# Attention and a mixture of experts on one core: all products of the attention in 64 x 32 tiles of the array

## The chip, the core and the metric

The kernel runs on one core of a Trainium2 chip. The metric is the device time of one execution in microseconds: 1344.58 before, the median of three runs (1342.93 to 1349.27).

## The reference

For 16 batches of 256 rows of 128 features:

```
x = x + tanh(g_xattn) * attn(layernorm(x), ctx)   # 16 heads of 8, softmax over 1601 keys per batch
x = x + tanh(g_ffn)   * ffn(layernorm(x))         # 8 experts 128 -> 512 -> 128, best 2 per token

attn: qh = q Wq[h]; kh = ctx Wk[h]; vh = ctx Wv[h]
      out_h = softmax(0.125 * qh kh^T) vh;  concat(out_h) Wo^T
ffn:  probabilities of the 2 best experts, normalised; sum of cw_e * (gelu(x w1_e^T + b1_e) w2_e^T + b2_e)
```

Everything is float32. The scores are large, so the maximum over the keys of every row and head is subtracted before the exponential.

## The kernel before

**Packing.** Queries and keys are split into three bfloat16 parts each. Six products of parts, of 8 features each, stand under one another on 48 partitions (`MAXROW`), for one head from partition 0 and for another from partition 64 (`RG` = 2 row halves of the array). Three more rows carry the negative maximum, so that a product of 51 rows gives score minus maximum.

**Work of a group.** Four heads are a group (`NG` = 4 groups a batch, 64 in all; `JJ` = 2 heads on each row half). A group needs:
- its maxima first: a *window* (`window`, L782) is a product of 128 queries with 402 keys (`WIN`), written into one bank of PSUM. The two row halves write the two banks of one buffer (`mxp`, `MX_BUFS` = 2), and DVE takes both banks in one reduction (`maximum`, L1540, L1546). `NMX` = 16 such pairs are a group. Then DVE joins them to `nmx` (L1554), POOL splits that in three (`split_maxima`), PE turns it (`turn_maxima`, L827), ACT copies it and two DMAs put it under the queries (`place_half`).
- 13 *units*, one per 128 keys (the last has 65). `scores` (L758) makes four products of 128 keys x 256 queries, two heads a bank, into a ring of three banks `st`, which also serves all smaller products; ACT makes the exponentials into SBUF (L1077); `weighted` (L803) multiplies them, four heads as four strips of 32 columns over all 128 key rows, by the values and a column of ones, and adds up in one bank `pv` over two groups. The values are float32, and each float32 product shows as two passes in the trace.

**Order.** Every engine runs a list written out by hand. PE's goes unit by unit: scores of this unit with the first pair of windows beside them, then further windows, the weighted values of the unit two before (`LAG`), then the chores that the tables at L96 to L106 put at this unit (keys', values' and queries' products of later batches, the attention's projection and the routing of the batch before), and last the windows of the second list. `WINDOWS_AT` (L108; `FIRST_WINDOWS_AT` for batch 0) says how many pairs are made at each unit, before and after the chores; `FIRST` pairs are made before the first unit and `LEAD` is how far the windows are ahead of the units. DVE takes reductions and its small work in the same order, ACT exponentials and copies. PE waits for a free `mxp` buffer (`s_red`), for a free ring bank (`freed`) and for the exponentials (`s_exp`); DVE waits for the windows (`s_mxp`), ACT for the scores (`s_st`) and for the weighted values (`s_pv`) before it writes over old exponentials.

After the last unit comes the expert stage: 43 blocks of rows, two products each with gelu between, and the sum of the results. The change does not touch it, except for the last transpose of the weighted values.

## Time and profile before

| | |
|---|---|
| median of the runs | 1344.58 us |
| span of the profiled execution, which is all that the page gives of its time | 1360.3 us |
| PE busy | 1289.7 us (95%), 14041 matmuls |
| DVE busy | 1157.6 us (85%) |
| ACT busy | 1094.7 us (80%) |
| POOL busy | 546.7 us (40%) |
| mean granted TensorE clock | 0.975 |

PE is TensorE's matmuls and PEld its weight loads, DVE is VectorE, ACT ScalarE, POOL GpSimd. A matmul's end is modelled, and matmuls are pipelined: PE's busy share says that something was in the array, not that it ran at its peak. Distances between starts say more.

### The profile page before, as it was taken

The page shows a single profiled execution, that of the slowest core. Times are in us where ns is not written, and L with a number is a line of the kernel's source. Part 1 is how long each engine was busy: PE and PEld are TensorE (multiplying, and loading weights), DVE is VectorE, ACT ScalarE, POOL GpSimd, SP SyncE. Part 2 cuts the span into 40 slices and gives each one's busy share as a digit, 9 for nine tenths or more (in the row PEclk, how much of TensorE's full clock was granted, in tenths as well). Part 3 has the DMA queues.
Part 4 walks back from the last instruction along what each step waited for, and adds up shares of the span by engine and source line. Part 5 has one row for each costly group of instructions (what it writes and reads, how often), then busy time and mean ns, then how long its engine had stood idle before and what let it go on. Part 6 is the DMA issues. An engine that isn't in the chain of part 4 may idle for free.

```text
span 1360.3 us, 38009 instructions
## 1 busy us (share of the span) xinstructions
PE 1289.7 (95%) x14041; PEld 627.0 (46%) x14041; DVE 1157.6 (85%) x2268; ACT 1094.7 (80%) x2190; POOL 546.7 (40%) x1208
## 2 busy tenths in 40 slices
PE   4899999999999999999999999999999999998992
PEld 2243444444444444444444444444444433497882
DVE  7897999999999999999999999999999999355334
ACT  1487898988889888898989898888989888864561
POOL 3231426262626262535353444444453512145441
PEclk7698999999999999999999999999999999999997
DMA  3232121212121212121222222222211110386886
GB/s 91 76 86 82 45 67 51 70 47 75 46 78 42 83 35 66 52 64 54 64 59 60 63 58 66 58 64 58 67 52 39 49 40 6 98 258 196 252 262 231
DMA packets 61077, 112.67 MB, mean 83 GB/s; under 512 B 13052, under 2 KB 36476, under 8 KB 60748
## 3 DMA queue, kind: packets, MB, share of 16 engines
q1 hardware_dynamic: 54043, 97.67, 24.6%
q0 software_dynamic: 4320, 8.99, 2.0%
q10 hardware_dynamic: 2529, 3.58, 0.8%
q8 instruction: 112, 1.84, 0.6%
q14 instruction: 73, 0.60, 0.2%
HBM read 52.77 MB, written 13.71 MB: 49 GB/s over the span
## 4 chain that ended last, share of the span: by engine, by line
PE 75%; DVE 16%; SPq 3%; issue 3%; DMA 1%; ACT 1%; POOL 0%; POOLq 0%; ACTq 0%; DVEq 0%
PE pv L821 27%; PE st L772 14%; PE mxp L794 13%; DVE mx L1546 13%; PE st L1038 5%; PE mxp L1048 4%; PE st L879 4%; PE st L888 2%; SPq L401 2%; PE st L900 1%; PE st L851 1%; PE st L923 1%; PE st L863 1%; PE st L933 1%; DVE x_sb L1741 1%
## 5 line engine op out<-in xcount | busy, mean ns | idle before, releaser
L1546 DVE TENSOR_REDUCE mx<-mxp 128x2 f32<-128x804 f32 x1024 | 985.2, 987 | 71.1 <-PE mxp L794 60.8
L1077 ACT ACTIVATE arena<-st 128x512 f32<-128x512 f32 (+1 forms) x1664 | 892.2, 595 | 88.8 <-PE st L772 82.2
L821 PE MATMUL pv<-arena 128*32 128x256 f32 x6656 | 535.6, 394 | 0.5 <-ACT pv_sb L1084 0.4
L794 PE MATMUL mxp<-kpack,qpack 48*128 48x402 bf16 x2048 | 457.0, 344 | 16.2 <-DVE mx L1546 14.8
L772 PE MATMUL st<-qpack,kpack 51*128 51x256 bf16 (+1 forms) x3328 | 449.2, 273 | 2.4 <-DMA qpack<-mxT 2.1
L772 PEld LDWEIGHTS st<-qpack,kpack 51*128 51x128 bf16 (+1 forms) x3328 | 199.4, 97 | 202.4 <-ACT arena L1077 108.0
L794 PEld LDWEIGHTS mxp<-kpack,qpack 48*128 48x128 bf16 x2048 | 142.6, 93 | 167.0 <-DVE mx L1546 94.3
L821 PEld LDWEIGHTS pv<-arena 128*32 128x32 f32 x6656 | 131.6, 108 | 177.0 <-issue 89.3
L659 POOL CAST mxs<-nmx 128x8 bf16<-128x8 f32 x64 | 12.4, 193 | 263.3 <-DVE nmx L1554 263.2
L1218 ACT ACTIVATE arena<-st,bias 128x256 f32<-128x256 f32 (+1 forms) x172 | 74.1, 438 | 54.7 <-PE st L1038 38.4
L702 POOL DMA_INDIRECT results<-ysb,idx x71 | 68.9, 971 | 89.2 <-DVE ysb L1683 58.2
L692 POOL DMA_INDIRECT rows<-xrow,pos x64 | 66.2, 1034 | 95.3 <-DVE pos L1403 80.0
L1038 PE MATMUL st<-xT,arena 128*128 128x256 f32 (+1 forms) x344 | 93.0, 353 | 12.1 <-ACT xT L1205 7.9
L1048 PE MATMUL mxp<-arena 128*128 128x128 f32 x568 | 90.8, 275 | 0.0
L1048 PEld LDWEIGHTS mxp<-arena 128*128 128x128 f32 x568 | 85.4, 191 | 5.6
L583 POOL TENSOR_TENSOR tmp<-rstd 128x2 f32<-128x2 f32 x93 | 18.1, 195 | 151.9 <-DVE rstd L1276 147.0
L1675 DVE TENSOR_TENSOR ysb<-mxp,arena 128x256 f32<-128x256 f32 (+1 forms) x43 | 16.3, 378 | 72.5 <-PE mxp L1048 65.8
L879 PE MATMUL st<-arena,wk_sb 128*128 128x400 f32 (+1 forms) x126 | 60.5, 566 | 5.7 <-DMA arena<-in_ctxT 5.7
L888 PE MATMUL st<-wv_sb,arena 128*128 128x128 f32 (+1 forms) x416 | 62.2, 289 | 0.0
L888 PEld LDWEIGHTS st<-wv_sb,arena 128*128 128x128 f32 (+1 forms) x416 | 49.6, 187 | 25.1 <-ACT arena L1119 13.1
L1038 PEld LDWEIGHTS st<-xT,arena 128*128 128x128 f32 x344 | 52.1, 191 | 17.4 <-ACT xT L1205 11.7
L634 POOL TENSOR_TENSOR ksp<-kf,ksp 128x400 bf16<-128x400 f32 (+1 forms) x60 | 56.9, 949 | 4.8
(194 smaller groups left out, 908.7 us busy)
## 6 DMA issues: line engine op xcount, KB each, us to landing
kpack<-ksp SPq DMA_DIRECT2D x750, 50.0 KB
arena<-in_w12T SPq DMA_DIRECT2D x43, 576.0 KB
arena<-in_ctxT SPq DMA_DIRECT2D x15, 800.5 KB, 4.5
qpack<-qsp SPq DMA_DIRECT2D x187, 32.0 KB
xblk<-rows SPq DMA_DIRECT2D x28, 132.0 KB
rows<-in_pads SPq DMA_DIRECT2D x8, 264.0 KB
arena<-results SPq DMA_DIRECT2D x8, 256.0 KB, 6.9
arena<-results ACTq DMA_DIRECT2D x8, 256.0 KB, 7.2
```

What stands on the lines that cost most here:

```text
L692: eng.indirect_dma_start(rows, bass.IndirectOffsetOnAxis(ap=pos[:, k, t:t + 1].bitcast(U32), axis=0), xrow[:, t, k, :], None).then_inc(don ...
L702: eng.indirect_dma_start(results, bass.IndirectOffsetOnAxis(ap=idx[:, i % IDX_BUFS, j:j + 1].bitcast(U32), axis=0), ysb[:, i % YS_BUFS, j, ...
L772: ins = eng.matmul(ring[i][0:n, jj * N:(jj + 1) * N], kpack[rows, b % 2, g * JJ + jj, kt * P:kt * P + n], qpack[rows, b % 2, g * JJ + jj, ...
L794: eng.matmul(mxp[pair % MX_BUFS][:, rg, 0:WIN], qpack[rows, b % 2, g * JJ + jj, t * P:(t + 1) * P], kpack[rows, b % 2, g * JJ + jj, WSTART ...
L821: ins = eng.matmul(pv[32 * j:32 * j + 32, 0:N], vaug[0:n, b % 2, kt, at:at + 32], pt[0:n, (2 * u + rg) % PT_BUFS, jj * N:(jj + 1) * N], st ...
L879: eng.matmul(dst[:, 0:kn], wk_sb[:, :], ctx_sb[:, b % 2, k0:k0 + kn], start=True, stop=True).then_inc(s_kp, 1)
L888: ins = eng.matmul(ring[i][0:n, t * D:(t + 1) * D], ctx_sb[:, b % 2, (t0 + t) * P:(t0 + t) * P + n], wv_sb[:, :], start=True, stop=True)
L1038: eng.matmul(hp[q % HP_BUFS][:, 0:n], w1[:, i % W_BUFS, c * P:(c + 1) * P], xT[:, i % 2, 0:n], start=True, stop=True).then_inc(s_hp, 1)
L1048: ins = eng.matmul(yp[i2 % 2][:, j * D:(j + 1) * D], hf[:, f % RING, j * P:(j + 1) * P], w2[:, i2 % W_BUFS, c2 * D:(c2 + 1) * D], start=(c ...
L1077: eng.activation(pt[0:n, c % PT_BUFS, :], ring[bank_of["S", u, p]][0:n, :], ACT.Exp, scale=SCALE).then_inc(s_exp, 1)
L1218: eng.activation(hf[:, q % RING, 0:n], hp[q % HP_BUFS][:, 0:n], ACT.Gelu_apprx_tanh, bias=bias[:, i % BIAS_BUFS, c:c + 1]).then_inc(s_hg, 1)
L1546: eng.tensor_reduce(mx[:, tj, w, :], mxp[windows_done % MX_BUFS][:, :, 0:WIN], AX.X, ALU.max).then_inc(s_red, 1)
```

## The change

- The tile of the array is named at every product. `strips` cuts a product into pieces of 32 output columns, each with its own load. Scores and windows become products of 64 x 32 tiles, on either row half; the products over 128 rows (keys, values, queries, projection, routing) become strips of 128 x 32.
- The weighted values are cut into the two halves of the 128 keys (`HALVES`), each in 64 x 32 tiles, and each half adds up in its own bank `pv[h]`. ACT copies both banks, and `turn_heads` transposes and adds them by two products with the identity, where it used the transpose mode.
- A window is 512 keys and one bank. Three make 1536 keys; the last 65 keys of all four head-and-half combinations of a row half go into one bank together (`REST`). `mxp` is three single banks, and DVE reduces each bank by itself: 13 pairs a group (`NMX`), 26 reductions.
- `s_mxp`, `s_st` and `s_pv` become two semaphores each, one for a row half. The tables of the order are written anew; `FIRST` goes from 24 to 17 and `LEAD` from 30 to 22.

PSUM stays at eight banks: 3 + 3 + 2 instead of 3 + 4 + 1.

```diff
-WIN = 402
-WSTART = [0, 400, 800, M - WIN]
-NW = len(WSTART)
+WIN = 512
+NF = M // WIN
+REST = M - NF * WIN
+NW = NF + 1
-NMX = JJ * NT * NW
+NMX = JJ * NT * NF + 1
-MX_BUFS = 2
+MX_BUFS = 3
+HALVES = ((0, RSTEP), (RSTEP, P))
+STRIP = 32
-K_AT = {1: 0, 4: 1, 5: 2, 6: 3}
-V_AT = {25: 0, 26: 1, 27: 2, 28: 3}
+K_AT = {1: 0, 4: 1, 5: 2, 8: 3}
+V_AT = {25: 0, 26: 1, 27: 2, 30: 3}
-FIRST, LEAD = 24, 30
-WINDOWS_AT = ("1011011110111111111111101001101110011111110111100111",
-              "1101111020000000000001101211100011100000011000120000")
+FIRST, LEAD = 17, 22
+WINDOWS_AT = ("0111111121010111101011111110111110110111101111111101",
+              "0000100001000000010001000010000010010000100000000001")
...
+            def strips(dst, weights, moving, row=0, **flags):
+                m = weights.shape[1]
+                for c in range(0, m, STRIP):
+                    n = min(STRIP, m - c)
+                    ins = eng.matmul(dst[c:c + n, :], weights[:, c:c + n], moving,
+                                     tile_position=(row, c), **flags)
+                return ins
...
-                    ins = eng.matmul(ring[i][0:n, jj * N:(jj + 1) * N],
-                                     kpack[rows, b % 2, g * JJ + jj, kt * P:kt * P + n],
-                                     qpack[rows, b % 2, g * JJ + jj, :],
-                                     start=True, stop=True)
+                    ins = strips(ring[i][0:n, jj * N:(jj + 1) * N],
+                                 kpack[rows, b % 2, g * JJ + jj, kt * P:kt * P + n],
+                                 qpack[rows, b % 2, g * JJ + jj, :],
+                                 rg * RSTEP, start=True, stop=True)
...
-                if pair >= MX_BUFS:
-                    eng.wait_ge(s_red, pair - MX_BUFS + 1)
+                n = RG * pair + 1 - rg
+                if n >= MX_BUFS:
+                    eng.wait_ge(s_red, n - MX_BUFS + 1)
-                eng.matmul(mxp[pair % MX_BUFS][:, rg, 0:WIN],
+                if m < NMX - 1:
+                    ins = strips(mxp[n % MX_BUFS][:, 0:WIN], ..., rg * RSTEP, start=True, stop=True)
+                else:
+                    for tj in range(NT * JJ):
+                        ins = strips(mxp[n % MX_BUFS][:, tj * REST:(tj + 1) * REST], ...,
+                                     rg * RSTEP, start=True, stop=True)
+                ins.then_inc(s_mxp[rg], 1)
...
-                for j in range(HG):
-                    ins = eng.matmul(
-                        pv[32 * j:32 * j + 32, 0:N], vaug[0:n, b % 2, kt, at:at + 32],
-                        pt[0:n, (2 * u + rg) % PT_BUFS, jj * N:(jj + 1) * N],
-                        start=first, stop=last, tile_position=(0, 32 * j))
-                ins.then_inc(s_pv, 1)
+                for h, (lo, hi) in enumerate(HALVES):
+                    keys_in = slice(lo, min(hi, n))
+                    for j in range(HG):
+                        ins = eng.matmul(
+                            pv[h][32 * j:32 * j + 32, 0:N], vaug[keys_in, b % 2, kt, at:at + 32],
+                            pt[keys_in, (2 * u + rg) % PT_BUFS, jj * N:(jj + 1) * N],
+                            start=first, stop=last, tile_position=(lo, 32 * j))
+                    ins.then_inc(s_pv[h], 1)
...
                 for t in range(NT):
-                    ins = eng.transpose(ring[i][:, t * P:(t + 1) * P],
-                                        pv_sb[:, k % 2, t * P:(t + 1) * P], id_sb[:, :])
+                    for h in range(RG):
+                        ins = eng.matmul(ring[i][:, t * P:(t + 1) * P],
+                                         pv_sb[:, k % 2, h, t * P:(t + 1) * P], id_sb[:, :],
+                                         start=h == 0, stop=h == RG - 1)
...
-                eng.tensor_reduce(mx[:, tj, w, :], mxp[windows_done % MX_BUFS][:, :, 0:WIN],
-                                  AX.X, ALU.max).then_inc(s_red, 1)
+                for rg in (1, 0):
+                    src = mxp[(RG * windows_done + 1 - rg) % MX_BUFS]
+                    eng.wait_ge(s_mxp[rg], windows_done + 1)
+                    if m < NMX - 1:
+                        eng.tensor_reduce(mx[:, tj, w, rg:rg + 1], src[:, 0:WIN], AX.X, ALU.max).then_inc(s_red, 1)
+                    else:
+                        eng.tensor_reduce(mx[:, :, NF, rg:rg + 1], src[:, 0:NT * JJ * REST] ...)
```

## Rows read from the trace of the kernel before

**Rows 1.** The page: busy times, PE by slices, two of the costliest groups.
```profile
PE 1289.7 (95%) x14041; PEld 627.0 (46%) x14041; DVE 1157.6 (85%) x2268; ACT 1094.7 (80%) x2190; POOL 546.7 (40%) x1208
...
PE   4899999999999999999999999999999999998992
...
L1546 DVE TENSOR_REDUCE mx<-mxp 128x2 f32<-128x804 f32 x1024 | 985.2, 987 | 71.1 <-PE mxp L794 60.8
L1077 ACT ACTIVATE arena<-st 128x512 f32<-128x512 f32 (+1 forms) x1664 | 892.2, 595 | 88.8 <-PE st L772 82.2
```
**Rows 2.** Stretches: length; busy (instructions) PE, PEld, DVE, ACT, POOL; clock; DMA; GB/s.
```profile
47.00:129.30 82.30, 78.73 (x799) 29.57 (x796) 67.89 (x88) 62.04 (x120) 20.86 (x50) 0.88 0.27 78
...
623.90:694.50 70.60, 70.26 (x819) 30.93 (x816) 66.39 (x120) 62.88 (x123) 31.08 (x74) 1.00 0.21 60
...
1117.40:1180.60 63.20, 60.26 (x714) 23.46 (x711) 45.02 (x107) 56.09 (x112) 15.95 (x39) 1.00 0.04 13
1180.60:1360.30 179.70, 143.24 (x1020) 131.47 (x1016) 79.05 (x347) 89.37 (x225) 72.78 (x75) 0.95 0.79 243
```
**Rows 3.** PE in order of time: start, us, what, number merged.
```profile
599.78 0.40 PE L821 MATMUL pv<-arena 128*32 128x256 f32 x4
...
604.31 0.27 PE L772 MATMUL st<-qpack,kpack 51*128 51x256 bf16 x1
604.51 0.64 PE L821 MATMUL pv<-arena 128*32 128x256 f32 x8
605.08 0.28 PE L772 MATMUL st<-qpack,kpack 51*128 51x256 bf16 x1
605.09 0.34 PE L794 MATMUL mxp<-kpack,qpack 48*128 48x402 bf16 x1
...
605.58 0.64 PE L821 MATMUL pv<-arena 128*32 128x256 f32 x8
```
**Rows 4.** PE in order of time, two pairs of windows after a values' product.
```profile
659.95 0.52 PE L794 MATMUL mxp<-kpack,qpack 48*128 48x402 bf16 x4
```
**Rows 5.** Weight loads in order of time; in brackets idle before and its releaser.
```profile
604.51 0.16 PEld L821 LDWEIGHTS pv<-arena 128*32 128x32 f32 x8 [0.21 <-ACT arena L1077]
605.08 0.09 PEld L772 LDWEIGHTS st<-qpack,kpack 51*128 51x128 bf16 x1 [0.41 <-ACT arena L1077]
...
658.86 0.97 PEld L888 LDWEIGHTS st<-wv_sb,arena 128*128 128x128 f32 x8 [0.41 <-issue]
```
**Rows 6.** DVE in order of time, beginning of batch 8.
```profile
626.86 1.90 DVE L1546 TENSOR_REDUCE mx<-mxp 128x2 f32<-128x804 f32 x2 [0.62 <-PE mxp L794]
...
629.17 1.89 DVE L1546 TENSOR_REDUCE mx<-mxp 128x2 f32<-128x804 f32 x2
...
635.79 4.66 DVE L1546 TENSOR_REDUCE mx<-mxp 128x2 f32<-128x804 f32 x5 [0.29 <-PE mxp L794]
...
645.57 0.16 DVE L1271 TENSOR_SCALAR half<-var 128x2 int32<-128x2 int32 x1
645.63 0.99 DVE L1546 TENSOR_REDUCE mx<-mxp 128x2 f32<-128x804 f32 x1
```
**Rows 7.** DVE in order of time, first and last of 18 with routing between.
```profile
665.02 0.99 DVE L1546 TENSOR_REDUCE mx<-mxp 128x2 f32<-128x804 f32 x1
...
671.57 0.98 DVE L1546 TENSOR_REDUCE mx<-mxp 128x2 f32<-128x804 f32 x1
```
**Rows 8.** ACT in order of time.
```profile
654.16 1.09 ACT L1077 ACTIVATE arena<-st 128x512 f32<-128x512 f32 x2
```
**Rows 9.** PE in order of time, after a wait in batch 0.
```profile
108.16 0.52 PE L772 MATMUL st<-qpack,kpack 51*128 51x256 bf16 x4 [2.06 <-DMA qpack<-mxT]
```
**Rows 10.** Stretches, with columns as in rows 2: batch 0, expert stage.
```profile
110.00:119.00 9.00, 9.00 (x63) 2.63 (x62) 5.58 (x9) 4.73 (x9) 0.79 (x4) 0.52 0.35 90
119.00:129.00 10.00, 9.84 (x123) 3.76 (x123) 9.05 (x10) 8.82 (x18) 2.14 (x4) 1.00 0.27 112
...
1240.00:1300.00 60.00, 53.33 (x385) 49.41 (x384) 25.27 (x116) 33.20 (x87) 29.84 (x31) 1.00 0.78 233
```

More of the change, by code:

```diff
@@ L264, in build @@
         xnT = sb("xnT", [P, N])
[L265 removed]
+        pv_sb = sb("pv_sb", [P, 2, RG, N])
         conc = sb("conc", [P, NT, HG, NG, DH])
@@ L385, in build, with scored, weighed @@
         block = ctx.enter_context(nc.Block())
+        def scored(eng, n):
+            for rg in range(RG):
+                eng.wait_ge(s_st[rg], n)
+        def weighed(eng, n):
+            for h in range(RG):
+                eng.wait_ge(s_pv[h], n)
         def load_results(eng, k):
@@ L746, in _ @@
             for part in range(1, 2 * NT):
-                eng.wait_ge(s_pv, (B - 1) * UNITS + ROWS_AT[part])
+                weighed(eng, (B - 1) * UNITS + ROWS_AT[part])
                 write_rows(B - 2, part, s_sc)
@@ L755, in _ @@
         def _(eng):
-            freed = [(s_k3, c + 1) for c in range(ST_BUFS)] + [(s_pvs, COPIES)]
+            def strips(dst, weights, moving, row=0, **flags):
[5 more added lines that the diff above has]
+                return ins
+            freed = [(s_k3, c + 1) for c in range(ST_BUFS)] + [(s_pvs, RG * COPIES)]
             def scores(u, rg, beside):
@@ L862, in queries @@
                 eng.wait_ge(s_xnT, b + 1)
-                eng.matmul(dst[:, 0:N], wq_sb[:, :], xnT[:, :], start=True, stop=True
-                           ).then_inc(s_qp, 1)
+                strips(dst[:, 0:N], wq_sb[:, :], xnT[:, :], start=True, stop=True).then_inc(s_qp, 1)
             def keys(b, c):
@@ L878, in keys @@
                     eng.wait_ge(s_ctx_b, 16)
-                eng.matmul(dst[:, 0:kn], wk_sb[:, :], ctx_sb[:, b % 2, k0:k0 + kn],
-                           start=True, stop=True).then_inc(s_kp, 1)
+                strips(dst[:, 0:kn], wk_sb[:, :], ctx_sb[:, b % 2, k0:k0 + kn],
+                       start=True, stop=True).then_inc(s_kp, 1)
             def values(b, c):
@@ L887, in values @@
                     n = key_rows(t0 + t)
-                    ins = eng.matmul(ring[i][0:n, t * D:(t + 1) * D],
-                                     ctx_sb[:, b % 2, (t0 + t) * P:(t0 + t) * P + n],
-                                     wv_sb[:, :], start=True, stop=True)
+                    ins = strips(ring[i][0:n, t * D:(t + 1) * D],
+                                 ctx_sb[:, b % 2, (t0 + t) * P:(t0 + t) * P + n],
+                                 wv_sb[:, :], start=True, stop=True)
                     if t == tn - 1:
@@ L922, in project @@
                 for t in range(NT):
-                    ins = eng.matmul(ring[i][:, t * P:(t + 1) * P], concT[:, t * P:(t + 1) * P],
-                                     wo_sb[:, :], start=True, stop=True)
+                    ins = strips(ring[i][:, t * P:(t + 1) * P], concT[:, t * P:(t + 1) * P],
+                                 wo_sb[:, :], start=True, stop=True)
                 ins.then_inc(s_f3p, 1)
@@ L932, in route @@
                 for t in range(NT):
-                    ins = eng.matmul(ring[i][:, t * NE:(t + 1) * NE], xn2T[:, t * P:(t + 1) * P],
-                                     rw_sb[:, :], start=True, stop=True)
+                    ins = strips(ring[i][:, t * NE:(t + 1) * NE], xn2T[:, t * P:(t + 1) * P],
+                                 rw_sb[:, :], start=True, stop=True)
                 ins.then_inc(s_rp, 1)
@@ L945, in rank_tokens @@
                 dst = ring[i][:, 0:NT * NE]
-                eng.matmul(dst, tri_bf[:, :], mask[:, :, :].rearrange("p t e -> p (t e)"), start=True, stop=False)
-                eng.matmul(dst, ones_bf[:, :], before[:, :, :].rearrange("p t e -> p (t e)"), start=False,
-                           stop=True).then_inc(s_rk, 1)
+                strips(dst, tri_bf[:, :], mask[:, :, :].rearrange("p t e -> p (t e)"), start=True, stop=False)
+                strips(dst, ones_bf[:, :], before[:, :, :].rearrange("p t e -> p (t e)"), start=False,
+                       stop=True).then_inc(s_rk, 1)
                 freed[i] = s_rkc, b + 1
@@ L1023, in turn_in @@
                 ins.then_inc(s_xtp, 1)
-            eng.wait_ge(s_red, GROUPS * NMX)
+            eng.wait_ge(s_red, RG * GROUPS * NMX)
             turn_in(0)
@@ L1080, in copy_weighted @@
             def copy_weighted(k):
-                eng.wait_ge(s_pv, 2 * KT * (k + 1))
+                weighed(eng, 2 * KT * (k + 1))
                 if k > 1:
                     eng.wait_ge(s_f1p, k - 1)
-                eng.activation(pv_sb[:, k % 2, :], pv[:, 0:N], ACT.Copy).then_inc(s_pvs, 1)
+                for h in range(RG):
+                    eng.activation(pv_sb[:, k % 2, h, :], pv[h][:, 0:N], ACT.Copy).then_inc(s_pvs, 1)
             def copy_rows(b):
```

85 lines of the change are left out of this document (47 added, 38 removed).

## The prediction

> **What bounds the kernel now.** I read the page's first two parts first: PE is busy 95% of the span and DVE 85%, and PE's digits are 9 from the second slice into the last stage [rows 1]. The stretches come next, cut where a batch's first exponential starts. Batches 1 to 14 take 70.6 us each ((1117.4 - 129.3) / 14) and look alike: PE 70.26 of 70.60 us, DVE 66.39, ACT 62.88 [rows 2]. Batch 0 takes 82.3 us, the last 63.2, the expert stage 179.7, and 47.0 us lie ahead of batch 0.
>
> Busy shares don't say who is late, so I go to starts. A plain unit of the PE queue has four score matmuls, one pair of windows and eight weighted passes (a fp32 matmul is two passes). One such unit's passes start at 604.51 and the next at 605.58 [rows 3]: 1.07 us. In it:
> - scores and windows run side by side on the two row halves of the array (605.08 and 605.09) and take the 0.41 us that the next two points leave of 1.07. 256 bf16 columns take 0.11 us, 402 take 0.18 (0.52 for two in a row less 0.34 for one) [rows 3, 4].
> - weighted: two passes 0.24 us apart (0.64 us for eight less 0.40 for four), four strips at once [rows 3]. With the second pass it ends at 604.99, 0.48 us.
> - holes: 604.31 + 0.11 = 604.42 to 604.51, and 604.99 to 605.08. Each is 0.09 us. The weight loads stand idle for 0.21 and 0.41 us there, put down to ACT or to issue in turn [rows 5], though they come at every unit with the same length.
>
> The last point is the change's lever. Scores and windows use half the rows with all columns, weighted all rows with 32 columns. The Trainium skill (TensorEngine Tiling (Array Packing), Tiling Modes) says that changing the tiling mode drains the engine. The two 0.09 us holes are what this trace has for that.
>
> DVE next. Its window reductions run back to back in places: two in 1.89 us where one is 0.987, so one every 0.90 us [rows 6]. A two-element operation lets the next start after 0.06 (645.57 to 645.63) [rows 6]; I take 0.065 as the fixed part of any, which leaves (0.90 - 0.065) / 804 = 1.04 ns an element. From 665.02 to 671.57 there are six reductions and eleven small operations: 6.55 - 6 x 0.90 = 1.15, so 0.10 us for each small one [rows 7]. A batch has 64 reductions (57.7 us) and some 56 others (5.6 us, and 0.9 for the larger ones and for four drains ahead of nmx): 64.2 us needed in 70.6. DVE idles 6.4 us a batch (its busy time of 66.39 counts a tail of 0.08 at each reduction that the next one overlaps, so it shows less).
>
> ACT: two exponentials in 1.09 us, one is 0.595, so 0.495 each back to back [rows 8]. 104 are 51.5, and with some 18 copies 59 us a batch.
>
> So PE bounds a batch at 70.6, but DVE stands at 64.2 behind it. What PE gains can be used only down to DVE's floor, and the change moves that floor.
>
> **DVE, the next bound.** A window is now 512 columns of one bank and one reduction; before, one took two banks of 402. A group has 3 x 4 windows on each row half and one rest of 4 x 65: 24 reductions of 512 and two of 260, where there were 16 of 804. Elements: 12,808 against 12,864, no gain. Instructions: 26 against 16, each with 0.065 fixed. 512 x 1.04 + 65 = 0.598 us; 260 x 1.04 + 65 = 0.336. A batch: 96 x 0.598 + 8 x 0.336 = 60.1 us, +2.4. A reduction of 512 isn't in the trace. With 0.06 as the fixed part a batch is 59.9 us, with the 0.10 of the mixed small operations (and 0.995 ns an element) 61.2. I take 0.065, the smaller end, as the next reduction waits for nothing of the one before it, which the small ones partly do. With the other 6.5 us the floor is 66.6.
>
> **PE.** Strips of 32 columns quadruple the instructions, but four strips run at once as the weighted ones do today (four are over 0.40 us after the first began [rows 3]), so stream time stays.
> - Scores 2 x 0.11 on either half; windows now one pair per unit on average (13 x 4 in 52 units, before 64): 0.22 for 512 columns; weighted two passes, 0.45 with the first load. Sum 0.88 us, both 0.09 holes gone. From below 0.86 (no load shows); from above, the halves of weighted and the windows get in each other's way because the queue is in order. If each half waited for the other for one pass, 0.22 more: 1.10. If the two halves of the keys didn't overlap at all, 0.45 more: 1.33. That two row halves run at once is shown for scores and windows, that four column strips do is shown for weighted, both together by no row. I take 0.90.
> - Chores. 70.6 - 52 x 1.066 = 15.2 us a batch for the keys', values' and other products and twelve second windows (some 3 us). These are 128-row products: they still change the mode, and they take the same passes. The heads' transpose turns from two matmuls into eight passes. Eight values passes with eight loads end 1.09 us after they begin (658.86 to 659.95) [rows 4, 5], so +0.7 us, twice a batch. 15.2 - 3 + 1.4 + 1 (switches that more places now see) = 14.6, from 12 to 18.
> - Sum 52 x 0.90 + 14.6 = 61.4 us (57 to 75). PE falls behind DVE.
>
> The instruction stream is the unknown. A batch has now 819 matmuls and 816 loads [rows 2] and then about 2,400 of each: scores 16 a unit, weighted 16, windows 128 a group, and 200 for the rest. At 70 us that is one instruction every 15 ns. In the trace four matmuls and eight loads of weighted come off the queue within 0.05 us [rows 5], some 4 ns each, but that is a queue that had filled; over a whole unit the trace shows 28 in 1.07 us, 38 ns each, with the array as the limit. So between 4 ns (0.3 us a unit, nothing) and 38 ns (182 us a batch). I take the fast end: after the 2.06 us wait at 108.16 the four score matmuls came together within 0.52 us, with the clock just falling [rows 9, 10], so nothing trickled in one by one; but nothing there asks for one every 15 ns either. The Trainium skill (TensorE: Matmul & The Clock Gate, "Wait — 56ns, not 53.3ns?") gives a floor of about 25 ns from matmul to matmul, and 62 ns where the sequencer's firmware decodes them. By the first a batch would want 60 us, still hidden, and by the second 149, both estimates; no row here shows either.
>
> **ACT.** Each pair of groups is copied from two banks, not one: two more copies of 0.39 a batch, 60 us. It stays behind DVE.
>
> **DVE's idle time after.** Floor 66.6, PE 61.4, ACT 60. PE has 5 us in hand, but in units with values or keys it still spends 1.7 to 2.1 us between two pairs of windows. The three single banks hold 1.8 us of DVE work, as the two double ones do now. A dozen such places at some 0.2 us: 2.2 us idle, 68.8 us a batch. Ends: 0.5 (67.1) and the 6.4 of today (73.0).
>
> **The sum**, against the profiled span of 1360.3:
> - 14 batches x (70.6 - 68.8) = -25.2
> - batch 0: windows made ahead 17 instead of 24, lead 22 instead of 30, so 57 pairs in it instead of 70; DVE 57 x 1.196 = 68.2 instead of 63.1, PE 78.7 of 82.3 today at a clock of 0.88 [rows 2]. The clock and the DMA wait stay: -4
> - last batch: 30 pairs instead of 34, few chores. PE 60.3 of 63.2 [rows 2], then 52 x 0.64 + 30 x 0.22 + 8 = 48; ACT 51.5 + 5 = 56.5 is the bound: -6.5
> - ahead of batch 0: 24 x 0.90 = 21.6 becomes 17 x 1.196 = 20.3: -1.3
> - expert stage: untouched but for one heads' transpose: 0
> Sum -37.0, span 1323.3. The page gives no time around the span; the median of the runs, 1344.6, is 1.2% below it, so -36.6 there: **1308 us**.
>
> **Rivals.**
> 1. *DVE takes all of it, slower.* The +2.4 us of reductions a batch stand; if PE still comes late at chores so that DVE idles as today (6.4), a batch is 73.0: 14 x 2.4 = +34, less 10 at the ends: 1368. It turns at 4.0 us of idle a batch. For: DVE idles now at those very places, 0.62 us at 626.86 and 0.29 at 635.79, between keys' products [rows 6]; eighteen of the fifty-two units have two pairs or none. Against: through 665 to 671, where PE has room, DVE doesn't idle at all [rows 7]. 17%, half of it (idle from 4 to 5 us) within what can be told from no change.
> 2. *The instruction stream, slower.* PE's sequencer can't give an instruction every 15 ns for long. It decides from 14.7 ns (70.6 us over 4,800). At 20 ns a batch is 96 us: 1344.6 + 15 x 25 = 1720. 8%. The Trainium skill's 62 ns, 149 us a batch by that estimate, would make it 2,500.
> 3. *The clock.* PE now waits for DVE some 8 us a batch. After the 2.06 us wait at 108 the clock fell to half and batch 0 paid for it (0.52 in 110 to 119, 1.00 in the ten after) [rows 9, 10]. Once in each of the 14 batches at 5 us (half of such a ten) is +70 on the forecast: 1378. Against: PE's waits will be of 0.3 us, and the expert stage keeps 1.00 at 53.3 us of 60 [rows 10]. 3%.
> 4. *No overlap of the halves.* PE 1.33 a unit, 69 + 14.6 = 84 us a batch: 1530. 4%.
> 5. *DVE nearly closed* (idle 0.5): 14 x 3.5 + 12 = -61: 1284. 8%, beyond the forecast's own range of 1290 to 1330 (60%).
>
> Faster: forecast, rival 5 and the mildest part of rival 1 (0.02): 0.70. Same, within 0.5% (6.7 us, what a measurement can tell from no change): 0.08. Slower: 0.22. The range is 1282 to 1360; beyond it lie rivals 2 to 4 (15%) and the ends of 1 and 5 (5%).
>
> **What would show it.** DVE busy over 92% of a middle batch, PE's weight loads waiting for mx by hundreds of ns a unit, batches 68 to 70 us apart. Reductions of 512 start 0.60 us apart; 0.63 or more puts 3 us on a batch. The 0.09 holes between the last score and the first weighted pass gone. Two weighted halves starting within 0.05 us of each other; a full pass apart speaks for the 1.10. PE starts spaced evenly at over 10 ns with "issue" before them, DVE idle, would be rival 2. A granted clock under 1.00 in a middle batch would be rival 3. The forecast is wrong if PE or ACT is last in the middle batches.

## The result, and the profile after

The changed kernel takes 1432.26 us (median of four, 1425.23 to 1439.63), the kernel before beside it 1345.68. The ratio is 1.065, interval 1.061 to 1.070: slower, where 1308 was predicted. The profiled execution is the fastest of the four, 1425.23 us, with a span of 1423.4. Of all executions below one is slow, of f2_proj_wide at 3963 us, and its ratio leaves it out.

The page of the changed kernel: busy times, PE by slices, the chain of waits, and the groups that answer to [rows 1]. In the second line each digit is PE's busy share of a fortieth of the span, in tenths.
```profile
PE 1308.0 (92%) x38937; PEld 777.8 (55%) x38937; DVE 1185.2 (83%) x2908; ACT 1083.6 (76%) x2222; POOL 542.9 (38%) x1208
...
PE   6899999999999999999999999999999999899992
...
PE 59%; DVE 35%; issue 4%; DMA 1%; ACT 1%; POOL 0%; SPq 0%; POOLq 0%; DVEq 0%
...
L1587 DVE TENSOR_REDUCE mx<-mxp 128x1 f32<-128x512 f32 x1536 | 964.3, 680 | 87.4 <-PE mxp L776 85.5
L1114 ACT ACTIVATE arena<-st 128x512 f32<-128x512 f32 (+1 forms) x1664 | 876.3, 605 | 165.9 <-PE st L776 154.1
```
Its stretches, with the columns of [rows 2] and cut in the same way: batch 0, batch 8, the last batch, the expert stage.
```profile
44.20:126.00 81.80, 76.15 (x2345) 41.20 (x2337) 69.40 (x130) 61.86 (x122) 20.66 (x50) 0.96 0.30 90
660.50:737.20 76.70, 71.39 (x2380) 40.02 (x2372) 68.14 (x160) 61.87 (x125) 30.85 (x74) 1.00 0.20 58
...
1186.20:1252.00 65.80, 59.91 (x2011) 32.77 (x1995) 48.54 (x134) 56.69 (x114) 15.21 (x39) 1.00 0.05 14
1252.00:1423.40 171.40, 142.54 (x1068) 131.56 (x1068) 79.04 (x347) 93.19 (x226) 72.09 (x75) 0.94 0.82 255
```
No engine is full any more. PE is busy 71.39 of 76.70 us, DVE 68.14, ACT 61.87. A middle batch takes (1186.2 - 126.0) / 14 = 75.7 us against 70.6: 14 x 5.1 = 72. Batch 0 is 0.5 shorter [rows 2], the last 2.6 longer, 2.8 less lie ahead, and the expert stage is 8.3 shorter in this execution; other kernels here with the same stage show 168 to 179, so I read nothing into that. Sum 63, the difference of the spans. The medians differ by 87: the profiled execution of the changed kernel is its fastest, and that of the kernel before (span 1360.3) is longer than any execution timed beside it.

The weight loads name what PE waits for. The first group of the changed kernel's loads of windows:
```profile
L776 PEld LDWEIGHTS mxp<-kpack,qpack 48*32 48x32 bf16 x8192 | 188.0, 91 | 247.7 <-DVE mx L1587 205.3 <-issue 24.8 <-DMA qpack<-qsp 0.8
```
PE waits 205 us for DVE to free a bank, DVE waits 85 us for PE to fill one, and ACT 154 us for PE's scores (82 before [rows 1]). They take turns. DVE's reductions run at the predicted pace:
```profile
711.98 1.28 DVE L1587 TENSOR_REDUCE mx<-mxp 128x1 f32<-128x512 f32 x2
```
Two end 1.28 us after the first began, one is 0.68: 0.60 apart. Adding up starts over nine to twelve middle batches (each operation counted as its duration less the 0.08 tail), DVE has 65.6 us of work a batch and 10.0 idle; before it had 63.5 and 7.1. The count moves by some 0.3 us with a tail of 0.07.

### The profile page after: what moved, and what is told of

The parts are those of the page before. It is cut to its first block, busy times and chain, and to the rows that moved or that the text cites. A ratio compares the mean times of both kernels' runs of the same rounds, so it can differ in the third digit from the quotient of the medians.

```text
span 1423.4 us, 88476 instructions
## 1 busy us (share of the span) xinstructions
PE 1308.0 (92%) x38937; PEld 777.8 (55%) x38937; DVE 1185.2 (83%) x2908; ACT 1083.6 (76%) x2222; POOL 542.9 (38%) x1208
## 3 DMA queue, kind: packets, MB, share of 16 engines
q8 instruction: 306, 5.01, 1.5%
## 4 chain that ended last, share of the span: by engine, by line
PE 59%; DVE 35%; issue 4%; DMA 1%; ACT 1%; POOL 0%; SPq 0%; POOLq 0%; DVEq 0%
DVE mx L1587 30%; PE pv L857 19%; PE st L776 17%; PE mxp L776 11%; PE st L1075 5%; PE mxp L1085 4%; PE st L936 2%; DVE bst L1295 1%; DVE x_sb L1785 1%; ACT arena L1114 1%; PE mxp L1059 1%; PE st L870 1%; DVE mx L1589 0%; DVE conc L1626 0%; DMA xblk<-rows 0%
## 5 line engine op out<-in xcount | busy, mean ns | idle before, releaser
L1587 DVE TENSOR_REDUCE mx<-mxp 128x1 f32<-128x512 f32 x1536 | 964.3, 680 | 87.4 <-PE mxp L776 85.5
L857 PE MATMUL pv<-arena 64*32 64x256 f32 x13312 | 631.5, 379 | 8.9 <-issue 8.3
L776 PE MATMUL mxp<-kpack,qpack 48*32 48x512 bf16 x8192 | 550.7, 339 | 57.1 <-DVE mx L1587 45.5
L776 PE MATMUL st<-qpack,kpack 51*32 51x256 bf16 x13056 | 595.9, 272 | 6.8 <-issue 4.6
L776 PEld LDWEIGHTS st<-qpack,kpack 51*32 51x32 bf16 x13056 | 254.7, 90 | 164.2 <-ACT arena L1114 60.6
L776 PEld LDWEIGHTS mxp<-kpack,qpack 48*32 48x32 bf16 x8192 | 188.0, 91 | 247.7 <-DVE mx L1587 205.3
L857 PEld LDWEIGHTS pv<-arena 64*32 64x32 f32 x13312 | 281.0, 106 | 53.1 <-issue 46.8
L776 PE MATMUL st<-arena,wk_sb 128*32 128x400 f32 (+1 forms) x504 | 57.8, 528 | 4.9 <-DMA arena<-in_ctxT 4.9
L776 PE MATMUL st<-wv_sb,arena 128*32 128x128 f32 (+1 forms) x1632 | 58.8, 276 | 0.0
L644 POOL TENSOR_TENSOR kf<-kf,ksp 128x400 f32<-128x400 f32 (+1 forms) x60 | 56.8, 946 | 5.0
```

Of the source, the lines that this page charges most:

```text
L644: eng.tensor_tensor(kf[:, cols], kf[:, cols], ksp[:, 0, cols], ALU.subtract).then_inc(s_pool, 1)
L776: ins = eng.matmul(dst[c:c + n, :], weights[:, c:c + n], moving, tile_position=(row, c), **flags)
L857: ins = eng.matmul(pv[h][32 * j:32 * j + 32, 0:N], vaug[keys_in, b % 2, kt, at:at + 32], pt[keys_in, (2 * u + rg) % PT_BUFS, jj * N:(jj + ...
L1587: eng.tensor_reduce(mx[:, tj, w, rg:rg + 1], src[:, 0:WIN], AX.X, ALU.max).then_inc(s_red, 1)
```

## The experiments

The letters in the quoted expectations: A is the coupling of PE and DVE at the window banks; B, later F, the instruction stream; G the array's own time and the turns. "Period" below is the mean over batches 1 to 14, from one batch's first weighted load to the next one's, in the profiled execution. A plain unit is one with one pair of windows and no chore. f1_short leaves out most columns of the windows and of the weighted values, and the three kernels with "half" in their names leave out half of each window's maxima.

| kernel | us | ratio to before (95%) | period |
|---|---|---|---|
| before | 1345 to 1357 | | 70.6 |
| changed | 1432.3 | 1.065 (1.061-1.070) | 75.7 |
| e1_wide | 1417.3 | 1.053 (1.050-1.056) | 75.0 |
| f4_whole_keys | 1410.0 | 1.049 (1.046-1.051) | 74.5 |
| f2_proj_wide | 1426.4 | 1.058 (1.056-1.061) | 75.7 |
| e2_even | 1428.4 | 1.064 (1.059-1.069) | 75.3 |
| e4_behind | 1477.2 | 1.096 (1.091-1.100) | 79.5 |
| e3_half_reads | 1407.5 | 1.048 (1.045-1.051) | 74.0 |
| f3_wide_half | 1365.7 | 1.015 (1.013-1.017) | 72.1 |
| f1_short | 1442.9 | 1.071 (1.065-1.076) | 77.5 |
| g2_before_half | 1336.2 | 0.984 (0.982-0.986) | 69.5 |
| g1_split | 1392.9 | 1.028 (1.025-1.030) | 72.8 |
| g3_before_tiles | 1398.2 | 1.031 (1.028-1.033) | 73.2 |
| f5_wide_4banks | 1366.3 | 1.007 (1.004-1.009) | 71.1 |
| h2_tiles_4banks | 1355.7 | 1.007 (1.004-1.009) | 70.8 |
| h3_joined | 1348.3 | 1.002 (1.000-1.004) | 70.7 |
| h4_joined_tiles | 1348.1 | 1.001 (0.999-1.003) | 70.6 |
| h7_proj_strips | 1328.6 | 0.988 (0.985-0.991) | 69.2 |
| h8_joined_proj | 1321.3 | 0.982 (0.980-0.985) | 68.7 |

### Tiles undone, wholly and in part

e1_wide, from the changed kernel (f4_whole_keys is its first line alone, f2_proj_wide the second for the 128-row products alone):
```diff
-HALVES = ((0, RSTEP), (RSTEP, P))
+HALVES = ((0, P),)                      # one bank pv, 128 key rows
...
-                for c in range(0, m, STRIP): ... tile_position=(row, c)
+                return eng.matmul(dst[0:m, :], weights, moving, **flags)
```


> The changed kernel with its order, windows and banks, but no small tiles: scores and windows 64 rows x 128 columns, weighted values over all 128 keys in 128 x 32 tiles in one bank, projections in one piece. A third of the matmuls. Theory A (PE and DVE take turns waiting for each other because the order and three single banks can't carry DVE's 1.2 us a pair over the chores; the tiles themselves shorten a PE unit from 1.07 to under 0.96 us): without tiles PE is slower at every unit and the time rises, to 1460 to 1520 us. Theory B (the instruction stream or the small tiles cost the time): it falls, to 1345 to 1400 us.

> The changed kernel with only the weighted values back over all 128 keys in one bank: 16 instead of 32 instructions a unit, one copy less and the heads' products halved; two changes of the array's mode a unit come back (0.18 us). 3,900 instructions a batch instead of 4,760. Theory F: the blocks now allow 61 us a batch, and DVE's 67 to 69 or PE's 70 are next: 1340 to 1390 us. Theory G: PE's unit is 0.15 us longer, 1440 to 1480 us.

Without any tile the kernel still takes 1417: most of the loss needs no tiles. What is left in e1_wide is windows of 512, 26 reductions in three single banks, and the new order, and these alone cost 71 of the 87 us. f4_whole_keys, with all tiles but the halves of the keys, is 22 us faster than the changed kernel, though its plain unit is the longest (1.130 us; 1.111 in e1_wide, 1.066 before, 0.87 with the halves where nothing is waited for). Both times, 1417 and 1410, lie between the ranges of the two theories: neither was the whole of it.

> The changed kernel, with only the 128-row products (keys, values, queries, projection, routing, ranks) back in one piece of 128 columns; scores, windows and weighted values keep their tiles. A batch has 66 products less in strips, some 400 instructions of 4,760 fewer (8%); the array's mode changes stay as many. Theory F: 4 to 5 us a batch less, 1355 to 1385 us. Theory G: the strips of these products load faster (106 ns for 32 columns against 191 for 128), so this is the same or slower: 1430 to 1450 us.

1426.4 against 1432.3, intervals that touch: no verdict at this size.

### The order of the windows

e2_even puts one pair at every unit, e4_behind puts the first pair behind both scores:
```diff
+WINDOWS_AT = ("1" * UNITS, "0" * UNITS)
...
-                scores(u, 0, windows(u, 0)[:1])
-                scores(u, 1, [])
+                scores(u, 0, [])
+                scores(u, 1, [])                 # and then windows(u, 0)
```


> The changed kernel with one pair of windows beside the scores of every unit from batch 1 on, none after the chores (the totals of a batch and the first batch's lists stay). Theory A: the order matters; DVE gets 1.2 us of work in each unit, no unit asks for two pairs and none is empty, so DVE's 10 us of idle a batch shrink by 2 to 5 us: 1350 to 1400 us. Theory B (instructions): the order doesn't matter, 1420 to 1440 us.

> The changed kernel with the windows of the first list behind both score products of the unit, not between the two products of the first row half. Theory A: a window that waits for DVE holds back half a unit's scores today, so that ACT idles 10 us a batch; behind them the scores go out first, ACT and the weighted values run on: 1.5 to 4% faster, 1375 to 1410 us. Theory B: no change or slightly slower, as less runs side by side on the two row halves: 1425 to 1445 us.

An even order gives nothing (1428). Behind the scores the windows no longer run beside them and it costs 45 us, more than either theory had. I take that as a sign that PE's own time counts and that PE isn't far from its limit either; DVE's relief below tests it.

### DVE relieved

```diff
-eng.tensor_reduce(mx[:, tj, w, rg:rg + 1], src[:, 0:WIN], AX.X, ALU.max)
+eng.tensor_reduce(mx[:, tj, w, rg:rg + 1], src[:, 0:WIN // 2], AX.X, ALU.max)
```
e3_half_reads is this on the changed kernel, f3_wide_half on e1_wide; g2_before_half reads 201 of each 402 on the kernel before.

> The changed kernel, but each reduction of a 512-column window reads 256 columns only, so the maxima are taken over part of the keys; PE and ACT do all their work. DVE's need a batch falls by 96 x 256 x 1.04 ns = 25.5 us, to some 40 us. Theory A: DVE is out of the way, PE and ACT run at their own pace, 60 to 64 us a batch: 1190 to 1250 us. Theory B: PE's instructions bound it, a batch stays at 72 to 76 us: 1390 to 1430 us.

> The kernel without small tiles (1417 us) and each reduction of a window reading 256 of its 512 columns (maxima over part of the keys). If DVE and its turns with PE bound the version without tiles, the time falls to PE's own 70 us a batch or less: 1325 to 1350 us. If PE alone bounds it (longer windows, this order), it stays within 1% of 1417.

> The kernel before with reductions that read 201 of the 402 columns of each bank (the other half of the maxima's columns is left out of the computation): DVE is relieved of some 27 us a batch. If PE alone set the 70.6 us, as the prediction had it, the time stays within 1% of 1346. If turns between PE and DVE already cost something before, batches fall to 68 or less (1310). Theory A allows at most 2 us a batch here, since DVE's needed 64.2 stood 6.4 under the period.

The kernel before gains 1.1 us a batch from a DVE at 58% of the span (1.6% of its time, where 1% was allowed): PE bound it, as predicted, but for a small part. e1_wide gains 2.9 and stays above its forecast of 1325 to 1350; the changed kernel gains 1.7. So a DVE with plenty of time doesn't give PE's 61 us a batch either. In e3_half_reads the plain unit is right, 0.87 us. PE of e3_half_reads in order of time, two units' passes:
```profile
647.93 0.61 PE L857 MATMUL pv<-arena 64*32 64x256 f32 x16
648.37 0.28 PE L776 MATMUL st<-qpack,kpack 51*32 51x256 bf16 x4
648.38 0.39 PE L776 MATMUL mxp<-kpack,qpack 48*32 48x512 bf16 x4
...
648.81 0.69 PE L857 MATMUL pv<-arena 64*32 64x256 f32 x16
```
From 647.93 to 648.81; the sixteen passes of both halves take 0.61 us, and the next scores begin inside them, 0.44 after the first. The rest is lost elsewhere. The same stream, 20 us earlier:
```profile
629.77 0.39 PE L776 MATMUL mxp<-kpack,qpack 48*32 48x512 bf16 x4
629.78 0.39 PE L776 MATMUL st<-qpack,kpack 51*32 51x256 bf16 x8
629.99 0.61 PE L857 MATMUL pv<-arena 64*32 64x256 f32 x13
632.89 0.63 PE L857 MATMUL pv<-arena 64*32 64x256 f32 x2 [2.30 <-issue]
```
Thirteen of sixteen passes of one unit, then 2.3 us of nothing, with no semaphore between them. Such holes lie at other units in every batch: over ten middle batches unit 43 takes 0.872 us in the median and 3.74 in the worst, where before its like (unit 13, say) stays between 1.065 and 1.067.

The place of the holes tells what they are. PE's instructions reach it in blocks of 256 (see the last section). I numbered all matmuls, loads and instructions of the sequencer of PE in order of time from the start of the trace. In batches 1 to 14 I took the gaps of over 0.45 us between successive starts that no semaphore explains, and asked at which of the 256 places of a block each stands. In e3_half_reads 63 of 64 stand at one and the same place, and in the changed kernel 31 of 32: there one block ends and the next begins. The hole above is one of them. The edge of a block costs, against the mean of the 255 other places, 2.6 us a batch in the changed kernel, 5.2 in e3_half_reads, 1.9 in f2_proj_wide, 0.2 in f4_whole_keys, and under 0.1 before, in e1_wide and in f3_wide_half.

f1_short has windows and weighted values of 64 moving columns only, and reductions of 64:
```diff
-ins = strips(mxp[n % MX_BUFS][:, 0:WIN],
+ins = strips(mxp[n % MX_BUFS][:, 0:64],
...
-pv[h][32 * j:32 * j + 32, 0:N], vaug
+pv[h][32 * j:32 * j + 32, 0:64], vaug
```


> New theory F: a batch of the changed kernel has 4,760 PE instructions, and they are fetched in blocks of 256 that follow one another at 3.4 us or more, 3.9 in the middle, so that a batch can't be under some 73 us whatever the array does; the reductions that read half a window left it at 1407 us. This kernel keeps every instruction of the changed one but takes the array's work and DVE's away: windows and weighted passes have 64 moving columns instead of 512 and 256, a reduction reads 64. (Maxima and weighted values are left out for the other columns.) A PE unit's array time falls from 0.88 to some 0.4 us. Theory F: still 1360 to 1410 us. Theory G (array time or turns between PE and ACT bound it): the time falls with them, ACT's 60 us a batch are next: 1180 to 1260 us.

With far fewer columns through the array the batch got longer, 77.5, beyond the range of either theory. The clock fell too (0.65 granted in a stretch of 80 us in the middle), so the total doesn't separate the stream from the clock; the edges of the blocks cost 7.2 us a batch.

### The instruction stream by itself

g1_split is the kernel before with each weighted product in four pieces of 64 columns; g3_before_tiles is it with scores and windows in tiles.
```diff
-                for j in range(HG):
-                        pv[32 * j:32 * j + 32, 0:N], vaug[...], pt[..., jj * N:(jj + 1) * N],
+                for c, j in ((c, j) for c in range(0, N, 64) for j in range(HG)):
+                        pv[32 * j:32 * j + 32, c:c + 64], vaug[...], pt[..., jj * N + c:jj * N + c + 64],
```


> The kernel before with one edit: each weighted product's 256 moving columns are cut into four products of 64 columns, so a unit has 32 weighted passes instead of 8 and a batch about 2,070 matmuls and as many loads in place of 819, with the same columns through the array, no window, reduction, bank or wait changed. Theory F (instructions reach PE in blocks of 256, one per 3.3 us or more, and PE runs dry where it takes them faster): 4,140 instructions in 70.6 us are 17 ns each; batches stay regular and within 2 us of 70.6 if the pieces cost no array time, and single stalls of 1 to 3 us inside a group of passes, with no semaphore, appear where many small products come together; gaps over 0.3 us without a wait rise from 1.36 us a batch to 2 or more. If each small product costs array time by itself, every plain unit grows by the same amount, without gaps. Theory A (the loss of the changed kernel is only the coupling of PE and DVE): nothing of both, 70.6 us a batch, 1346.

> The kernel before with one part of the change: scores and windows in 64x32 tiles (four strips each, the tile named); windows of 402 columns in two double banks, the order, the reductions and the weighted values (128 rows x 32 columns) are those of before. About 28 matmuls a plain unit and 1,800 a batch. Theory A: array time and DVE's work are as before, so 1346 within 1%. Theory F: 3,600 instructions a batch, 20 ns each, some stalls, up to 1 us a batch: 1346 to 1365. A price of the strips themselves (loads that show) would be a longer plain unit, from 1.07 to 1.13 as in the changed kernel with weighted values over whole keys: 1390.

With the same columns through the array g1_split is 36 us slower. The plain unit grows by 0.022 us, 1.1 a batch. Unit 0 of each batch takes 2.03 us, 1.07 before, another 1.0. The edges of the blocks cost 0.3. PE of g1_split at unit 0:
```profile
633.04 0.43 PE L821 MATMUL pv<-arena 128*32 128x64 f32 x14
633.89 0.55 PE L821 MATMUL pv<-arena 128*32 128x64 f32 x18 [0.43 <-issue]
```
A single set of 32 passes that all wait for one semaphore, broken after the 14th. This hole does not stand at the edge of a block (it is 96 instructions away from the nearest), so by its place it is no wait for the next block, and its cause stays open.

g3_before_tiles was expected within 1%, at 1365 at most, or at 1390 with a plain unit of 1.13 us. It came out at 1398, with a plain unit of 1.084: 0.9 us a batch. The edges of its blocks cost nothing. The other 1.8 us lie in two units: unit 7 takes 2.40 us, 1.43 before, and unit 0 takes 1.92, 1.07 before. In unit 7 the loads of the scores stand for 0.84 us, put down to ACT; why they have to wait there, and not in the kernel before, is open. Unit 0 loses in both runs, which may have one cause.

### Banks and reductions

f5_wide_4banks gives e1_wide the bank that its single `pv` leaves free, h2_tiles_4banks does so to f4_whole_keys:
```diff
-MX_BUFS = 3
+MX_BUFS = 4
-        pv = [ps(f"pv{h}", [P, BLK]) for h in range(RG)]
+        pv = [ps(f"pv{h}", [P, BLK]) for h in range(1)]
```


> The changed kernel without tiles and with the weighted values over whole keys in one bank (1417 us, 75.1 a batch), and the bank that this sets free given to the windows: four single banks in place of three, 2.4 us of DVE's work ahead in place of 1.8. Theory A (turns: DVE drains its banks while PE does chores, PE then stands at a full bank) expects DVE's idle time to fall by a third, 73 to 74 us a batch, 1390 to 1400. If only the reductions' fixed cost counts, 1417 stays.

> The changed kernel with the weighted values over whole keys in one bank (1410 us, 74.4 a batch) and the freed bank given to the windows: four single banks. Without tiles the same edit took a batch from 75.1 to 71.1. Theory A (the loss is turns between PE and DVE at three single banks): the same 3 to 4 us a batch go here too, 70.5 to 71.5 a batch, about 1355 to 1370. Theory F (the instruction stream, some 3,800 instructions a batch): the gain is smaller, as single stalls appear where PE runs ahead; 72.5 or more, 1385.

This is the larger part of the cause. One more bank takes the period from 75.0 to 71.1 us, and from 74.5 to 70.8 with tiles; the time, from a ratio of 1.053 to 1.007 and from 1.049 to 1.007: in f5_wide_4banks about twice the gain a batch that was expected. PE's loads of windows wait 57 us for DVE, not 144, and DVE's reductions 28 for PE, not 78; by starts, DVE's idle time falls from about 9 to about 5 us a batch. First the two groups of e1_wide, then those of f5_wide_4banks:
```profile
L1584 DVE TENSOR_REDUCE mx<-mxp 128x1 f32<-128x512 f32 x1536 | 966.2, 682 | 83.3 <-PE mxp L775 78.4
L775 PEld LDWEIGHTS mxp<-kpack,qpack 48*128 48x128 bf16 x2048 | 153.3, 94 | 185.8 <-DVE mx L1584 143.8 <-issue 27.0 <-DVE mx L1586 0.2
```
```profile
L1584 DVE TENSOR_REDUCE mx<-mxp 128x1 f32<-128x512 f32 x1536 | 960.0, 683 | 38.2 <-PE mxp L775 27.7
L775 PEld LDWEIGHTS mxp<-kpack,qpack 48*128 48x128 bf16 x2048 | 149.2, 94 | 98.6 <-DVE mx L1584 56.5 <-issue 28.3 <-DVE mx L1586 0.4
```
How a turn looks: the weight loads of one and the same unit, first in e1_wide, then in f5_wide_4banks, while DVE reduces without a pause in both.
```profile
708.93 0.16 PEld L854 LDWEIGHTS pv<-arena 128*32 128x32 f32 x8 [0.21 <-ACT arena L1111]
709.50 0.09 PEld L775 LDWEIGHTS mxp<-kpack,qpack 48*128 48x128 bf16 x1 [0.41 <-DVE mx L1584]
709.88 0.09 PEld L775 LDWEIGHTS mxp<-kpack,qpack 48*128 48x128 bf16 x1 [0.30 <-DVE mx L1584]
709.89 0.32 PEld L775 LDWEIGHTS st<-qpack,kpack 51*128 51x128 bf16 x4
710.42 0.16 PEld L854 LDWEIGHTS pv<-arena 128*32 128x32 f32 x8 [0.21 <-issue]
```
```profile
673.49 0.16 PEld L854 LDWEIGHTS pv<-arena 128*32 128x32 f32 x8 [0.21 <-ACT arena L1111]
674.06 0.10 PEld L775 LDWEIGHTS mxp<-kpack,qpack 48*128 48x128 bf16 x2 [0.41 <-DVE mx L1584]
674.07 0.32 PEld L775 LDWEIGHTS st<-qpack,kpack 51*128 51x128 bf16 x4
674.60 0.16 PEld L854 LDWEIGHTS pv<-arena 128*32 128x32 f32 x8 [0.21 <-ACT arena L1111]
```
With three banks the second window of a pair finds no bank at 709.50, and the four score products stand behind it in the queue until 709.88; the unit takes 1.49 us, not 1.11. What PE loses here it can't give back, since DVE is full; at the next chore (2 us) DVE, with three banks of 0.60 us, runs dry and loses there. This last step is read from the sizes and not shown in lines. With four banks the pair goes out together.

h3_joined keeps the four banks but pairs them, with one reduction over both as before; h4_joined_tiles is it with the tiles of f4_whole_keys.
```diff
-                for rg in (1, 0):
-                    eng.tensor_reduce(mx[:, tj, w, rg:rg + 1], src[:, 0:WIN], AX.X, ALU.max)
+                src = mxd[windows_done % 2]
+                eng.tensor_reduce(mx[:, tj, w, :], src[:, :, 0:WIN], AX.X, ALU.max)
```


> The changed kernel without tiles, weighted values over whole keys, windows of 512 in two double banks, and one reduction over both banks of a pair as in the kernel before: 13 reductions a group in place of 26, 3.4 us less of DVE's work a batch than with single banks; PSUM's four window banks are those of the run with four single banks (1366 us, 71.1 a batch, against 1357 of before). Theory A with the fixed cost of 26 reductions as a part: DVE needs 63.2 in place of 66.6, a batch 69.5 to 70.5, 1340 to 1355. If the grain of the buffers counts more than the fixed cost (a double bank is free only when both halves are read), 71.5 or more, 1375.

> As the run with joined reductions, with scores, windows and projections in tiles and strips of 32 columns. Theory A: as the joined run without tiles, plus the 0.02 us that the tiles add to a plain unit, 1 us a batch: 1355 to 1365. Theory F: some 3,800 instructions a batch, single stalls; 1380 or more.

Ratios 1.002 and 1.001: twice as many reductions cost 0.4 us a batch at most once the banks are there, though joining them takes 3.2 off DVE's work (62.9 a batch by starts, 66.1 in f5_wide_4banks), because PE now sets the end: the chain is 88% PE and 4% DVE in h3_joined, 60% and 31% in f5_wide_4banks. Tiles with whole keys neither gain nor lose here; at 3,896 matmuls and loads a batch, 18.1 ns each, the edges of the blocks cost 0.2 us.

### The part worth keeping

h7_proj_strips is the kernel before with only the 128-row products in strips, h8_joined_proj is h3_joined with only these.
```diff
-eng.matmul(dst[:, 0:kn], wk_sb[:, :], ctx_sb[:, b % 2, k0:k0 + kn], start=True, stop=True)
+strips(dst[:, 0:kn], wk_sb[:, :], ctx_sb[:, b % 2, k0:k0 + kn], start=True, stop=True)
```


> The kernel before with one part of the change: the products over 128 rows (keys, values, queries, projection, routing) as strips of 128 x 32. Scores, windows, weighted values, banks, reductions and order are those of before. In the joined and four-bank runs a unit with a values product took 2.00 us in strips and 2.20 without, one with a first keys product 1.81 and 1.98, others up to 0.3 less, while the plain unit grew by 0.02 through the tiles of scores and windows, which this kernel doesn't have. Since PE sets the kernel before (70.6 us a batch), four values units at 0.2 and six others at 0.15 to 0.2 give 1.5 to 2 us a batch: 1345 - 15 x 1.75 = 1319, 1315 to 1330. Rival: the gain comes only where weighted values, scores and projections all have 32 columns, and the strips add loads: 1345 or more.

> The joined run (windows of 512 in double banks, one reduction for two banks, 1348 us) with strips in the projections alone, scores and windows wide. Plain units at 1.11 and values units at 2.00: 1.5 to 2 us a batch below the joined run's 70.75 and about 1.3 below the run with joined reductions and tiles everywhere: 69 us, 1320 to 1330. By the same rival: 1348.

Both beat the kernel before by little, but by more than the interval: 1328.6 (ratio 0.988, interval 0.985 to 0.991) and 1321.3 (0.982, interval 0.980 to 0.985). Where it comes from, a values unit of PE in h3_joined, then in h8_joined_proj:
```profile
653.05 0.64 PE L855 MATMUL pv<-arena 128*32 128x256 f32 x8
653.62 1.16 PE L776 MATMUL st<-wv_sb,arena 128*128 128x128 f32 x8
654.71 0.28 PE L776 MATMUL st<-qpack,kpack 51*128 51x256 bf16 x1
```
```profile
638.26 0.64 PE L859 MATMUL pv<-arena 128*32 128x256 f32 x8
638.72 1.06 PE L778 MATMUL st<-wv_sb,arena 128*32 128x128 f32 x32
639.71 0.28 PE L798 MATMUL st<-qpack,kpack 51*128 51x256 bf16 x1
```
The strips have the shape of the weighted values' tiles. They start 0.46 us after the weighted passes began, not 0.57, and the next scores follow after 0.99, not 1.09.

Not tried: halves of the keys with four window banks. All kernels here use eight banks, and this one would take nine (3 + 4 + 2), or both halves' sums in one. So the bank is shown by the relatives of the changed kernel, not in the changed kernel itself.

## Why the prediction was wrong

**The step that failed** is "DVE's idle time after": 2.2 us a batch predicted, 10.0 measured, with 0.5 to 6.4 given as the ends. That is 7.8 us a batch; the floor, 66.6 predicted, was 65.6. Together 68.8 + 7.8 - 1.0 = 75.6 for the 75.7 seen. Its reasoning has two errors; how the 7.8 us divide between them in the changed kernel itself no run separates:
- "The three single banks hold 1.8 us of DVE work, as the two double ones do now." True as a sum, but the kernel before had PE as its bound, with DVE 6 to 7 us behind it; a buffer that is enough there isn't enough where both have the same load. A fourth bank gave back 3.7 to 3.9 us a batch (f5_wide_4banks, h2_tiles_4banks). The bank had gone to `pv`.
- "PE has 5 us in hand", from PE at 61.4. With DVE's reading halved the changed kernel still takes 74.0 (e3_half_reads). The plain unit was right (0.87 for 0.90) but can't be kept up. The edges of the blocks cost 2.6 us a batch in the changed kernel and 5.2 in e3_half_reads, and the sum had the stream at nothing ("I take the fast end"). Beside a values product the halves gain nothing: the shortest unit with one takes 2.02 us in e3_half_reads and 2.00 in f4_whole_keys, though the plain ones take 0.87 and 1.13. So chores at 14.6 on top of 0.90 a unit were too low. The rest (PE waits for ACT's exponentials, and ACT 154 us for scores) isn't divided up.

Point by point:
- *Who bounds before.* Right: g2_before_half, 1.1 us a batch.
- *Reductions of 512 at 0.598.* Right: 0.60.
- *The holes of 0.09 go, both halves run at once.* Right: sixteen passes in 0.61 us (eight took 0.64 before [rows 3]), scores beginning inside them. The sign named for it, halves starting within 0.05 us of each other, is not met: the second half's first load starts 0.15 us after the first's in the median.
- *Small operations of DVE.* Between 665.02 and 671.57 there are ten, not eleven, so 0.115 us each and not 0.10; it puts 0.8 us on DVE's need before and after alike. The count by starts gives less than either, 63.5.
- *Batch 0 -4, last -6.5, ahead -1.3.* Batch 0 -0.5, last +2.6, ahead -2.8. The last batch has the same turns.
- *Rival 1*, DVE takes all at 6.4 us of idle (1368, 17%). The nearest of all (DVE idles at PE's chores), but mis-sized: the idle time of today was taken as its upper end, though the buffers changed with the load.
- *Rival 2*, the stream, decides from 14.7 ns. It exists above that pace, as single holes of up to 2.7 us instead of an even pace. At 16.0 ns (4,744 matmuls and loads in 75.7 us) it costs 2.6 us a batch; at 18.1 ns in h4_joined_tiles 0.2. The sign named for it (even starts over 10 ns apart) was the wrong sign to look for, and its price (96 us a batch at 20 ns) the wrong form.
- *Rivals 3 to 5.* Each ruled out: the granted clock stayed at 1.00 in the middle batches, the halves overlap, DVE idles more than before.

Seen from its parts: windows, reductions, banks and order +4.4 us a batch (e1_wide, of which 3.9 the missing bank and 0.4 the single reductions), tiles -0.5 (f4_whole_keys), halves of the keys +1.2. In that last term the edges of the blocks grow by 2.4 us, from 0.2 to 2.6; with no such stalls the halves would have gained about 1.2, by this subtraction.

## What to carry to other kernels

When a change moves the bound from one engine to another that is fed through a few buffers, don't price the buffers by how they did while one side had time in hand: with both sides near the same load each needs its slack, and one bank was worth over 4% here. Count what an edit takes from a shared pool before counting what it gives. Look at where holes stand in the order of instructions, and not only in time: that told the fetch from the waits here. And try each part by itself: the strips of the 128-row products alone gave 1.2%, under a change that as a whole lost 6.5%.

## What the runs showed of the hardware

**The stream of PE comes in blocks.** The queue that carries instructions moved 306 packets and 5.01 MB in the changed kernel, 112 and 1.84 MB before. Queue, packets, MB and share of the DMA engines, from the changed kernel's DMA view:
```profile
q8 instruction: 306, 5.01, 1.5%
```
One packet of 16 KB goes with 256 of PE's instructions. In the changed kernel these packets start 3.3 us apart at the least and 3.9 in the median (10.5 before), which is 13 ns an instruction at the closest seen. PE's own fastest 256 went at 8.9 ns each. The hole at 629.99 to 632.89 above stands at the edge of a block, and the packet before its end was under way from 630.59 to 631.47. So it is with the 31 such gaps of the changed kernel and the 63 of e3_half_reads: each ends 1.2 to 1.6 us after the last packet of this queue has landed. Place and time together show PE standing for its next block; no experiment changes the fetch alone. The Trainium skill (Runtime: NRT & Kernel Launch, Instruction fetch mechanics) has the 256-instruction blocks, which these traces agree with, and says that the fetch is hidden behind the issue of instructions; with these products the measurement differs.

**A half with one key row does not run beside the other.** The last unit of a group has 65 keys, 64 and one. Weight loads of the changed kernel there:
```profile
661.20 0.19 PEld L857 LDWEIGHTS pv<-arena 64*32 64x32 f32 x8
661.80 0.15 PEld L857 LDWEIGHTS pv<-arena 1*32 1x32 f32 x8 [0.41 <-issue]
```
The second half of the weighted values, a 1*32 form, starts 0.60 us after the first, with the 0.41 us of idle time that loads of another shape show too. Over all 64 such units it is 0.57 to 0.76; in the other units the second half's first load starts 0.15 us after the first's, in the median.

**Granted clock with short products.** f1_short, in which PE gives products of 64 columns for most of a batch, was granted 0.65 between 600 and 680 us, a mean of the two levels 1.2 and 2.4 GHz, where all others had 0.98 to 1.00.
